# Sixteen keys summed by four halving additions instead of one strided reduce, in the routed attention of an eight-image hybrid block

## What is computed

```python
_, r_idx = jax.lax.top_k(logit, TOPK)                      # 4 windows of 256
kv_sel = jax.vmap(lambda kvp, idx: kvp[idx])(kv_pix, r_idx)
attn = jax.nn.softmax(jnp.einsum('npmqc,npmkc->npmqk', qh * SCALE, k_sel), axis=-1)
out = jnp.einsum('npmqk,npmkc->npmqc', attn, v_sel)        # sum over the 16 keys
```

## Time and profile before

| what | value |
|---|---|
| median of 3 runs | 2231.73 us (2230.4 to 2237.41) |
| the profiled execution | 2236.57 us, span 2234.7 us |
| mean granted TensorE clock | 0.84 of full speed |
| L946, the sum over the keys | 64 instructions, 240.2 us busy |
| L939, the products before it | 64 instructions, 165.6 us busy |
| L915, sums of the key products | 112 instructions, 135.6 us busy |
| GpSimd: L1255 and L1252 (taps), L1239 (key products) | 505.1, 269.7 and 307.2 us busy |
| chain that ended last, by engine | PE 27%, issue 25%, DVE 22%, POOL 10% |

### The profile page before, as it was taken

The page is one execution under the profiler, slowest core; times in us unless marked ns, Lnnn a source line. Parts: engine busy times, 40 slices in busy tenths (PEclk is TensorE's granted clock), DMA queues, the critical chain, the costliest instruction groups (busy, mean ns, idle before and its releaser), DMA issues.

```text
span 2234.7 us, 38864 instructions
## 1 busy us (share of the span) xinstructions
PE 1614.0 (72%) x14592; PEld 1050.2 (47%) x14592; DVE 1541.2 (69%) x2668; ACT 929.0 (42%) x1273; POOL 1146.0 (51%) x582
## 2 busy tenths in 40 slices
PE   2004557886878767896778867797677868788897
PEld 1001235553556435563455534564355635565565
DVE  3893679657786678757696677856797586852564
ACT  0000137522664226631465226632275315653682
POOL 0994789045960579226880559505891369700000
PEclk9557779897889878998788978898788987899998
DMA  4201100030000300021000300012000300000000
GB/s 131 74 0 59 55 1 2 1 116 9 1 1 19 107 1 1 2 78 48 1 1 1 125 1 1 1 38 88 1 1 1 104 11 1 1 1 11 1 2 10
DMA packets 26162, 61.93 MB, mean 28 GB/s; under 512 B 4192, under 2 KB 13408, under 8 KB 25824
## 3 DMA queue, kind: packets, MB, share of 16 engines
q0 software_dynamic: 9216, 33.56, 4.5%
q1 hardware_dynamic: 16736, 25.60, 3.6%
HBM read 46.56 MB, written 12.58 MB: 26 GB/s over the span
## 4 chain that ended last, share of the span: by engine, by line
PE 27%; issue 25%; DVE 22%; POOL 10%; ACT 4%; DMA 2%; DVEq 1%; POOLq 0%; ACTq 0%; SPq 0%
POOL KV L1239 7%; PE psB L405 7%; DVE P L1048 6%; PE psB L536 5%; DVE Q L946 4%; POOL KVSEL L1226 2%; PE psB L554 2%; PE psA L585 2%; DVE PROD L939 2%; DVE STACKED L1097 2%; DMA window_table<-KV 2%; PE psB L514 2%; PE psB L502 1%; PE psB L528 1%; PE psB L519 1%
## 5 line engine op out<-in xcount | busy, mean ns | idle before, releaser
L1255 POOL TENSOR_TENSOR XLEPE<-XLEPE,KV 128x1024 f32<-128x1024 f32 x200 | 505.1, 2525 | 16.7
L536 PE MATMUL psB<-W,P 128*128 128x128 f32 x2048 | 317.0, 304 | 114.0 <-DVE NEGMAX L1048 106.5
L1239 POOL TENSOR_TENSOR KV<-KVSEL,Q 128x1024 f32<-128x1024 f32 x112 | 307.2, 2769 | 156.1 <-DVE KVSEL L915 120.1
L1048 DVE CUSTOM_DVE_ANT_0 P<-psB,W 128x1024 f32<-128x1024 f32 x256 | 312.6, 1221 | 72.3 <-PE psB L405 42.7
L727 ACT ACTIVATE P<-P,NEGMAX 128x1024 f32<-128x1024 f32 x256 | 293.1, 1145 | 128.5 <-DVE NEGMAX L1056 127.1
L536 PEld LDWEIGHTS psB<-W,P 128*128 128x128 f32 x2048 | 262.1, 157 | 179.7 <-issue 131.7
L1226 POOL DMA_INDIRECT KVSEL<-window_table,CHOSEN x64 | 60.8, 949 | 553.0 <-DMA window_table<-KV 508.7
L1252 POOL TENSOR_SCALAR KV<-V_PAD,W 128x1024 f32<-128x1024 f32 x200 | 269.7, 1348 | 72.3 <-POOL XLEPE L1255 39.8
L735 ACT ACTIVATE PT<-psB 128x1024 f32<-128x1024 f32 x256 | 260.1, 1016 | 65.9 <-PE psB L536 65.0
L405 PE MATMUL psB<-TN,W 128*128 128x512 f32 (+1 forms) x512 | 256.0, 635 | 12.2 <-DVEq L1100 9.5
L502 PE MATMUL psB<-H_PAD,DIAG 32*32 32x512 f32 x4608 | 188.8, 706 | 73.7 <-DVEq L1175 39.2
(11 more groups left out here) (119 smaller groups left out, 2109.4 us busy)
## 6 DMA issues: line engine op xcount, KB each, us to landing
window_table<-KV SPq DMA_DIRECT2D x8, 1024.0 KB, 5.8
X<-x_by_window_dram SPq DMA_DIRECT2D x8, 512.0 KB
XLEPE<-x_dram SPq DMA_DIRECT2D x8, 512.0 KB, 4.1
out_dram<-PT SPq DMA_DIRECT2D x8, 512.0 KB, 3.9
W<-packed_dram SPq DMA_DIRECT2D x1, 3714.5 KB, 11.6
KVSEL<-window_table,CHOSEN POOLq DMA_INDIRECT x64
FC<-packed_dram SPq DMA_DIRECT2D x8, 64.0 KB, 2.2
PROD<-gains_dram SPq DMA_DIRECT2D x1, 256.0 KB, 12.1
```

The lines of the kernel that those rows point to most:

```text
L536: mm = pe.transpose(ps[:, t * 128:(t + 1) * 128], P[:, i % P_BUFFERS, t * 128:(t + 1) * 128], ident)
L1048: dve.tensor_tensor_reduce(P[:, b, :], ps[:], w("band", at, at + TOK), 1.0, -3.0e38, ALU.mult, ALU.max, NEGMAX[:, b, 0:1]).then_inc(free, 1)
L1239: pool.tensor_tensor(PRODUCTS[i % 2].rearrange("p (k c) -> p k c", c=C), KVSEL[:, t, keys, 0:C], Q[:, t, q, :].unsqueeze(1).broadcast_to([ ...
L1255: pool.tensor_tensor(acc, acc, product, ALU.add).then_inc(lepe_done, 1)
```

## The change

`attend` adds the upper half of `PROD` to the lower half, contiguously, until one key's width is left: additions of 1024, 512, 256 and 128 elements per partition. The first three write in place, the last writes `Q`. Each waits for the one before. The count of marked instructions grows by three for each of the eight attends of an image.

```diff
-LINKS_A2 = 30
+LINKS_A2 = 30 + 3 * WTILES * PX
...
                 def attend(t, q):
-                    chain.settle()
-                    chain.mark(dve.tensor_reduce(Q[:, t, q, :], PROD[:].rearrange("p (k f) -> p f k", k=KEYS),
-                                                 AX.X, ALU.add))
+                    width = KEYS * C
+                    while width > C:
+                        width //= 2
+                        chain.settle()
+                        total = Q[:, t, q, :] if width == C else PROD[:, 0:width]
+                        chain.mark(dve.tensor_tensor(total, PROD[:, 0:width], PROD[:, width:2 * width], ALU.add))
                     if q == PX - 1:
                         chain.settle()
                         dve.sem_inc(pv_done, 1)
```

## The result

The changed kernel takes 2312.64 us (median of 4 runs, 2305.4 to 2319.85), the kernel before in the same measurements 2234.57: a ratio of 1.0345, 95% interval 1.0298 to 1.0392. By this ratio it is **slower by 77 us** (the two medians lie 78 us apart); 93 had been forecast. The profiled executions differ by 72.8 us (2309.37 against 2236.57).

What follows compares the result with a forecast made beforehand. VectorE was taken to bound the MLP stretch and dense attention, with GpSimd excluding its two-input additions. 7 images x (5.5 + 6.0) plus 12 for image 0 gave +93 us, 2325 us against the median; range 2262 to 2362.

Steps and rivals of the forecast that it cites:

- What bounds the stretches: MLP stretch and dense attention: VectorE time is kernel time, passed on whole in the first and nearly whole in the second.
- Additions free of GpSimd take 2.6 us: Each attend's sum: four additions take 2605 ns by their widths, against 3753 ns for the reduce.
- Who goes first: Shared SBUF port: between two adjacent VectorE instructions a waiting GpSimd instruction goes first, so four additions can wait four times.
- VectorE keeps its turn: Rival, both stretches: a following addition goes before the waiting GpSimd instruction; some +10 us, 2242; chance 0.08.
- the gain arrives: Rival, both stretches: additions do not contend, both inputs lying in one tile; 56 us faster, 2176; chance 0.07.
- the third attend caught: Rival, dense attention: a third attend per image also meets the taps; 7 x 5 = 35 us more, 2360; chance 0.08.
- the signs named: Changed profile: additions 1.7 to 2.7 us beside taps, MLP stretch 38.6 us, higher L1255 and L1252 means, longer L1048 waits.
- MLP stretch +5.5: First L939 to fc2 residual, per image: two full rounds +2.2 us each, the first +1.0, behind the last mv +0.15.
- Image 0 +12: Second half beside its own taps: the residual starts some 12 us later, 25 without the 13.5 us of cover.
- Dense attention +6.0 per image: Between the score units: two attends beside taps at +4.0 us, two free at -1.05, and 0.1 for the edge.
- the rival of absorption: Dense attention: score buffers and catching up behind a stall hide its part; +50 us, 2282; chance 0.15.

Runs made afterwards that it cites:

- short_adds: Changed kernel with GpSimd's key products and taps cut short, most of their work left out, all waits kept: 2034.42 us, 0.906 of the kernel before.
- t1_only: Kernel before with halving additions for tile 1 only, the strided reduce kept for tile 0: ratio 1.0153, 36 us slower.
- short_reduce: Kernel before, reduce kept, with GpSimd's key products and taps cut short, all waits kept: 2115.21 us, 0.943 of the kernel before.
- one_add: Kernel before with each sum as one addition of 1024 elements, then a strided reduce of eight keys: ratio 1.0074, 17 us slower.

## Why the prediction was right

- *What bounds the stretches.* Right: VectorE's time in the MLP stretch came through whole, +5.6 us in each of seven images.
- *Additions free of GpSimd take 2.6 us.* Right: 1220, 737, 425 and 292 ns in `short_adds`, 2.7 with their gaps.
- *Who goes first.* Right: the 128-element addition takes 2.31 us between taps, and the second addition is the slowest in the mean. "VectorE keeps its turn" and "the gain arrives" are both out, and so is the third attend caught: it takes 3.2 to 3.3 us. Of the signs named, one came only in part: GpSimd's tap addition (L1255, now L1258) was to have a higher mean than 2525 ns and has 2533, hardly more; the scaled copy has 1446 for 1348.
- *MLP stretch +5.5.* Measured 5.6, and the round 10.27 us for the 10.25 worked out.
- *Image 0 +12.* Its end (L984, now L987) moved from 189.31 to 201.38. A sum beside taps there takes 8.4 us, not 7.8, and seven of the eight meet them; the taps end at 195.4. To image 1's first product it is +13.5.
- *Dense attention +6.0 per image: mis-sized.* It is +2.9. The sums themselves came out nearly as put, 20.6 us per image against 15.4, +5.2. (These are VectorE's groups by line, summed over the seven stretches.) Of these VectorE got 0.9 back in L1066 (L1063 before), a copy that also waits for GpSimd (674 to 577 ns in the mean), some 0.3 in other instructions, and 1.1 in shorter idle time. I had taken every microsecond of VectorE there as kernel time, from its 92% of busy time. The number came out halfway between the forecast and the rival of absorption, but that rival's mechanism, score buffers that hide the stall, is not what the traces show. TensorE's waits for the score scaling grew by all of it, from 15.2 to 20.6 us per image, and all of TensorE's idle time by 5.4. What made up for 2.6 of that is TensorE's own work (means over the seven stretches): the same 873 matmuls were busy 89.0 us instead of 91.6. In both kernels the granted clock stood at its lower level, 1.2 GHz, for 23.9 us of a stretch in the mean; but TensorE was busy for 22.6 us of that before and for 16.4 after, so more of the slow time fell on waits. The low parts of image 4's stretch, added up, before and then after:

```profile
sum 23.90, PE 23.90 PEld 18.07 DVE 20.25 ACT 18.52 POOL 18.98; mean PE 3.41 PEld 2.58 DVE 2.89 ACT 2.65 POOL 2.71
```

```profile
sum 23.90, PE 15.48 PEld 11.77 DVE 20.17 ACT 11.28 POOL 18.96; mean PE 3.87 PEld 2.94 DVE 5.04 ACT 2.82 POOL 4.74
```

The longest low part there, 1180.6 to 1190.8, covers 4.9 of the 7.25 us that TensorE waits for the first sum. Eight transposes take 1.94 us at the lower level (the row at 1185.53 above) and 1.09 at the upper (the one at 1176.14). By these two, 6.2 us less of work at the lower level is an estimated 2.7 us saved, against the 2.6 measured. `t1_only` fits: waits +4.3, work at the lower level 2.1 us less, busy time 0.8 less, stretch +3.5. This is an accounting of the traces; no experiment sets the clock, and why the low parts fell on waits is open.

The sum by the measured terms is 7 x (5.6 + 2.9) + 13.5 = 73 where 93 was forecast. That term alone accounts for 22 us of the difference, and the others lean 2 us the other way.

## What to carry to other kernels

Price a VectorE instruction by its number of SBUF tensor inputs, not only by its elements, whenever GpSimd works beside it: a slow one-input reduce can be cheaper than four fast two-input additions, since each of them can wait for a whole GpSimd instruction and hold up the next. The number of inputs is not a complete test: the copy L1063 has one, and takes 674 ns in the mean beside GpSimd's full work and 227 in `short_reduce`. If the faster form is wanted, put it where GpSimd is idle, and look in the timeline whether it is.

## What I had not expected

Without GpSimd's hold the dense attention shrank by 7.0 us in the mean for 4.9 us less of VectorE. The stretch of one image in `short_reduce` and in `short_adds` (length, busy us of PE, PEld, DVE, ACT, POOL, then PEclk, the granted clock):

```profile
1008.85:1116.24 107.39, 87.67 (x873) 58.83 (x871) 90.69 (x149) 78.03 (x108) 4.03 (x13) 0.94 0.01 1
```

```profile
969.61:1069.60 99.99, 84.67 (x873) 56.89 (x871) 85.78 (x161) 77.82 (x108) 4.38 (x14) 0.97 0.01 1
```

TensorE was idle 4.4 us less, was granted 0.97 instead of 0.94 of its 2.4 GHz, and did the same matmuls in 3.0 us less. Why the clock was higher is not shown. The clock also scatters between kernels where nothing differs: between the end of the second-last dense attention and the last fc2 residual no product, sum or tap is left to run, yet the profile of before takes 93.77 us at 0.93 and that of `one_add` 100.55 at 0.85:

```profile
1976.05:2069.82 93.77, 80.72 (x875) 51.70 (x874) 30.10 (x124) 28.65 (x35) 0.00 (x0) 0.93 0.02 7
```

```profile
1991.64:2092.19 100.55, 87.61 (x875) 56.45 (x874) 30.11 (x123) 28.64 (x35) 0.00 (x0) 0.85 0.02 6
```

In the twelve profiles of this document that stretch takes 93.4 to 100.6 us. Some 7 us, 0.3%, of a difference between two single profiles of this kernel can thus be the clock.

The other was that a strided write costs VectorE about what a strided read does: 1.4 us for 2048 elements in steps of 16 (3.7 us against 2.29, both where no GpSimd instruction is met), 1.47 for reading them in steps of 128 (3753 ns in the mean against 2282).
